# Key-matrix products of an attention and expert kernel in three passes of rounded parts

## Chip, cores and metric

The kernel runs on one core of a Trainium2 chip. The metric is device time in microseconds (us) of one execution; lower is better. A core has five engines that run side by side, each through its own list of instructions in order: TensorE (PE; its weight loads are listed as PEld), VectorE (DVE), ScalarE (ACT), GpSimd (POOL), and SyncE (SP), which here only issues DMAs. They wait for each other through semaphores.

## The reference

Four batches of 1024 tokens of width 256 attend to 77 context rows each with 16 heads of 64; then a mixture of 9 experts (the best two per token) follows. Cut to what matters for this change:

```python
xn = layernorm(x, ln1_w, ln1_b)            # x: the context rows, 4 x 77 x 256
ln = layernorm(latents, ln2_w, ln2_b)      # latents: the normed tokens, 4 x 1024 x 256
q = ln @ Wq
k, v = jnp.split(xn @ Wkv, 2, axis=-1)
q = q * (1.0 + scale) + shift              # one scale and one shift for each batch and head
attn = softmax(einsum('bihd,bjhd->bhij', q, k) * 64 ** -0.5)
x = x + einsum('bhij,bjhd->bihd', attn, v) @ Wout
x = x + experts(layernorm(x))              # top 2 of 9, gate, up and down products
```

## The kernel before

All data are float32. Where products run on parts, a matrix is held as a rounded high part (type F32R) and the rest, its low part (also F32R), and `product` (L338 to L342) sums high x high, high x low and low x high, three matmuls.

The token side of the scores never forms q. Since q is linear in the normed token, Wq and the keys are multiplied beforehand into a key matrix `keymat` of 256 rows for each batch, head and context row, and the scores of a token tile are one product with it. In the same way v and Wout are multiplied into value matrices, which go through DRAM (`valmat_dram`) because they are needed in another layout. This preparation fills the first 75 us or so; then come 32 token tiles (`step(s, s)`, L1429), then the experts. The order of each engine's work is written out by hand.

The preparation in order, by what PE does:

- Context rows are normed and turned. For each of 8 head pairs c PE makes keys into banks 4 to 7 and values into banks 0 to 3 (L1237 to L1243). ACT copies each value block out (L975, L976; increments `prep_moved`). DVE makes `k_head` from the keys, four operations of 64x308 for each c (L1580, `keys_moved`): for each head, its own 64 rows times the scale, the other 64 rows times the shift. Ahead of pair 4 DVE also makes the matrix `mix` (L1564, L1567).
- PE turns Wout in four groups (L1250), which ACT empties (`empty`, L953). Every block of the phase goes through the banks 0 to 3 in turn, and `fill(n)` waits until ACT has emptied block n-4. The blocks are numbered: values 0 to 7, Wout 8 to 11, query weights 12 to 19.
- PE multiplies Wq by `mix` for each pair (L1259), with small side products (L1264, L1266). ACT moves the result into `wq_head` (L985), each head's own 64 rows; the other 64 rows hold 1/256 from a GpSimd memset (L793). It ends each pair with L988.
- The value and key stage. For m = 0 to 31 PE makes one key matrix block (L1310: one float32 matmul of `wq_head`, 128x128, with `k_head`, 128x308); the first 16 of them each follow a value block `val(m)` (L1283, float32, 64 rows). ACT rounds each key block to `keymat` high (L1022) and DVE subtracts for the low part (L1591); four banks are in turn. ACT and DVE move the value blocks in turn (L1001, L1610) into four staging buffers `val_st`, and SP stores each filled buffer to `valmat_dram` with two or three DMAs (L596). Eight stores are made in this stage. After them SP waits until all are written (L602), issues `load_valmat(0)` (L612, L614), and goes on.
- Eight more value blocks of 52 rows are staged in `late_f` and `valmat_f` (`late_vals`), four in the steps 0 and 1 each; DVE waits for all eight stores to be written before it moves the first (L1607).

Of the kernel before, what the change touches and what calls it, by code (L numbers as in the profile page):

```python
# [28 lines left out]
P = 128  # L29
# [14 lines left out]
BM = B * M  # L44
# [9 lines left out]
STATS_DONE = 4  # L54
VALS_FROM = 4
STORE_HEADS = 4
STORE_BUFFERS = 4
# [60 lines left out]
def program(nc, x, ctx_rows, fside, ln1_w, ln1_b, ln2_w, ln2_b, wq, wkv, wout, wr, wg, wu, wd, out):  # L118
# [3 lines left out]
    with ExitStack() as ctx:  # L122
# [3 lines left out]
        def sb(name, shape, dt=F32, on=ctx):  # L126
            return on.enter_context(nc.sbuf_tensor(name, shape, dt))
# [45 lines left out]
        most = sb("most", [P, E])  # L173

        xn = [sb(f"xn{i}", [P, 2, ROW]) for i in range(4)]
        gap = [sb(f"gap{i}", [P, 1]) for i in range(2)]
# [52 lines left out]

        wq_head = sb("wq_head", [P, PAIRS, 2, D], F32, prep)  # L230
        k_head = sb("k_head", [P, PAIRS, 2, BM], F32, prep)
        early = ExitStack()
        wkv_sb = sb("wkv_sb", [P, KT, 2 * INNER], F32, early)
# [4 lines left out]
        side_row = sb("side_row", [1, B * H], F32, early)  # L238
        c_parts = [sb(f"c_{n}", [P, KT, BM], F32R, early) for n in ("hi", "lo")]
        ln_cols = sb("ln_cols", [P, 4, KT], F32, early)  # L240
# [137 lines left out]
        keys_made = sem("keys_made")  # L378
        keys_moved = sem("keys_moved")
        val_made = sem("val_made")  # L380
        val_moved = [sem(f"val_moved{i}") for i in range(2)]
# [114 lines left out]
        def prep_bank(n):  # L496
            return bank[n % 4]
# [67 lines left out]
        def _(sp):  # L565
# [44 lines left out]
            def load_valmat(b):  # L610
# [3 lines left out]
                sp.dma_start(valmat_f[0:KLAST, b % 2, KC - 1, :], rows[(KC - 1) * P:]).then_inc(valmat_loaded, 16)  # L614

            load_valmat(0)
            for n in range(SOON_STORES, STORES):
# [142 lines left out]
        def _(pool):  # L760
# [31 lines left out]
            pool.wait_ge(wkv_split, len(KV_PIECES))  # L792
            nc.gpsimd.memset(wq_head[:], 1.0 / D).then_inc(halves_filled, 1)  # L793

# [154 lines left out]
        def _(act):  # L949
# [21 lines left out]
            for c in range(PAIRS):  # L971

                act.wait_ge(prep_made, PREP_V + c + 1)
                src = prep_bank(PREP_V + c)
                nc.scalar.activation(v_whole[:, :, c, :], src[:, 0:(CR - 1) * P].rearrange("p (r n) -> p r n", n=P), ACT.Copy)  # L975
                nc.scalar.activation(v_last[:, c, :], src[:, (CR - 1) * P:BM], ACT.Copy).then_inc(prep_moved, 1)  # L976
            for n in range(4):
                half = slice(n % 2 * INNER // 2, (n % 2 + 1) * INNER // 2)
                empty(PREP_OUT + n, wout_t[:, n // 2, half], prep_bank(PREP_OUT + n))
# [229 lines left out]
        def _(pe):  # L1209
# [46 lines left out]
            for c in range(PAIRS):  # L1256
                to = fill(PREP_WQ + c)
                for k in range(KT):
                    nc.tensor.matmul(to[:, 0:D], wq_sb[:, k, c * P:(c + 1) * P], mix[:, k, :],  # L1259
                                     start=k == 0, stop=k == KT - 1)  # L1260
# [10 lines left out]
            def val(m):  # L1271
# [5 lines left out]
                if not m:  # L1277
                    pe.wait_ge(prep_moved, PREP)
                if m >= 2:
                    pe.wait_ge(val_moved[m % 2], (m - 2) // 2 + 1)  # L1280
# [18 lines left out]
            for m in range(MATS):  # L1299
# [8 lines left out]
                if m >= 4:  # L1308
                    pe.wait_ge(mat_lo, m - 3)
                nc.tensor.matmul(mat_bank(m)[:, 0:BM], wq_head[:, h // 2, h % 2, k * P:(k + 1) * P], k_head[:, h // 2, h % 2, :],  # L1310
                                 start=True, stop=True).then_inc(mat_made, 1)
            def scores(s, c, i):
# [192 lines left out]
        def _(dve):  # L1505
# [65 lines left out]
            for c in range(PAIRS):  # L1571
# [3 lines left out]
                for i in range(2):  # L1575
# [3 lines left out]
                    for rows, by in ((own, side_scale), (other, side_shift)):  # L1579
                        ins = nc.vector.tensor_tensor(k_head[rows, c, i, :].rearrange("p (b k) -> p b k", b=B), keys,  # L1580
                                                      by[own, :, 2 * c + i].unsqueeze(2).to_broadcast([DH, B, M]), ALU.mult)
                ins.then_inc(keys_moved, 1)

            def mat_rest(m):
# [483 lines left out]
```

## Time and profile before

| what | us |
|---|---|
| median of 3 timed runs | 855.67 (854.84 to 857.24) |
| the profiled execution, its own time | 854.76 |
| its span, first to last instruction | 853.1 |
| mean granted TensorE clock in it | 0.982 of full speed |

| engine | busy us (share of the span) |
|---|---|
| PE | 805.5 (94%) |
| DVE | 669.4 (78%) |
| ACT | 620.8 (73%) |
| POOL | 368.2 (43%) |

The profile is one execution. Its page gives the busy share of each engine, the clock that the throttle granted to TensorE (1.00 is full speed), the chain of work that ended last, and the costliest groups of instructions. The trace behind it can be asked for one stretch: instructions in order of time, the chain, groups by line and shape, and busy time by window. "Idle before it, releaser" says how long the engine had waited and which instruction's semaphore ended that. A float32 matmul shows as two records; one of an F32R operand as one. A busy share over the whole span is a mean over stages, and the preparation is a small one: what is read for this change is the first 92 us.

### The profile page before, as it was taken

What the parts mean: (1) busy time and instruction counts of PE and PEld (TensorE: products, weight loads), DVE (VectorE), ACT (ScalarE), POOL (GpSimd) and SP (SyncE); (2) the same over time, 40 slices, a digit from 0 to 9 for tenths busy, and PEclk for the clock granted to TensorE, in tenths of its full rate; (3) what the DMA queues carried; (4) which work ended last, traced back from release to release, by engine and by line L of the source; (5) the groups of instructions that cost most, each with busy time, mean ns of one, the idle gap of its engine ahead of it and who ended that gap; (6) DMA issues with size and microseconds to landing.
All of it is one profiled execution on the core that took longest, in us unless ns stands there. A gap on an engine that the chain in (4) does not pass through costs nothing.

```text
span 853.1 us, 19506 instructions
## 1 busy us (share of the span) xinstructions
PE 805.5 (94%) x6007; PEld 761.1 (89%) x6007; DVE 669.4 (78%) x1624; ACT 620.8 (73%) x1959; POOL 368.2 (43%) x534
## 2 busy tenths in 40 slices
PE   5999999999999999789699999999999999999993
PEld 4846899999999999789699999999999999999993
DVE  6667888889888887878578778888787888888771
ACT  4557989899889888535477777778777777777771
POOL 3020268677778766652133334233333222523232
PEclk9999999999999999879899999999999999999998
DMA  8044720310320020647547247246745565555212
GB/s 290 10 120 147 227 82 32 121 56 32 104 72 33 33 82 33 199 125 180 143 100 192 45 103 188 39 106 187 186 112 148 140 155 148 143 143 154 46 25 26
DMA packets 77675, 96.14 MB, mean 113 GB/s; under 512 B 10311, under 2 KB 64771, under 8 KB 77571
## 3 DMA queue, kind: packets, MB, share of 16 engines
q1 hardware_dynamic: 63811, 75.93, 29.4%
q0 software_dynamic: 13760, 18.96, 11.7%
q8 instruction: 48, 0.79, 0.4%
q14 instruction: 56, 0.46, 0.2%
HBM read 108.14 MB, written 31.29 MB: 163 GB/s over the span
## 4 chain that ended last, share of the span: by engine, by line
PE 84%; DMA 5%; SPq 3%; issue 2%; DVE 2%; ACT 1%; POOL 1%; DVEq 0%; POOLq 0%; ACTq 0%
PE banks L340 24%; PE banks L342 24%; PE banks L341 24%; PE banks L1327 4%; DMA valmat_dram<-val_st 2%; PE banks L1478 2%; PE banks L1341 2%; DMA expert_in<-blank 1%; SPq L596 1%; PE banks L1259 1%; PE banks L1283 1%; DMA tok<-expert_in 1%; PE banks L1295 1%; PE banks L1310 1%; DMA wkv_sb<-in_L_xattn_Wkv 0%
## 5 line engine op out<-in xcount | busy, mean ns | idle before, releaser
L340 PE MATMUL banks<-tok_t_hi,wgt_hi 128*128 128x256 f32 x704 | 202.2, 287 | 2.9 <-DVE hid_f L1947 2.5
L342 PE MATMUL banks<-tok_t_hi,wgt_lo 128*128 128x256 f32 x704 | 200.6, 285 | 0.0
L341 PE MATMUL banks<-tok_t_lo,wgt_hi 128*128 128x256 f32 x704 | 200.2, 284 | 0.0
L932 POOL DMA_INDIRECT result<-res,tok_id x72 | 117.6, 1634 | 184.5 <-ACT res L1162 154.0
L1032 ACT ACTIVATE prob<-banks,row_min 128x77 f32<-128x77 f32 x512 | 161.7, 374 | 5.7 <-DVE row_min L1674 5.7
L1939 DVE TENSOR_TENSOR wgt_lo<-wgt,wgt_hi 128x704 fp32r<-128x704 f32 x174 | 150.3, 904 | 14.7 <-ACT wgt_hi L1105 14.7
L340 PEld LDWEIGHTS banks<-tok_t_hi,wgt_hi 128*128 128x128 f32 x704 | 135.6, 193 | 5.3 <-issue 3.9
L341 PEld LDWEIGHTS banks<-tok_t_lo,wgt_hi 128*128 128x128 f32 x704 | 135.7, 193 | 0.0
L342 PEld LDWEIGHTS banks<-tok_t_hi,wgt_lo 128*128 128x128 f32 x704 | 135.6, 193 | 0.0
L1105 ACT ACTIVATE wgt_hi<-wgt 128x704 fp32r (+1 forms) x174 | 130.5, 800 | 0.5
L1032 ACT ACTIVATION_READ_ACCUMULATOR prob<-banks,row_min 128x1 f32 x512 | 130.7, 257 | 0.0
L340 PE MATMUL banks<-wgt_hi,hid_hi 128*128 128x256 f32 x360 | 105.0, 292 | 7.4 <-issue 6.1
L342 PE MATMUL banks<-wgt_hi,hid_lo 128*128 128x256 f32 x360 | 102.0, 283 | 0.0
L341 PE MATMUL banks<-wgt_lo,hid_hi 128*128 128x256 f32 x360 | 101.5, 282 | 0.0
L882 POOL TENSOR_TENSOR prob<-prob,row_inv 128x1232 f32<-128x1232 f32 x32 | 72.1, 2253 | 56.5 <-DVE row_inv L1688 56.4
L340 PE MATMUL banks<-valmat_hi,prob_t_hi 128*128 128x266 f32 x320 | 95.1, 297 | 0.7 <-DVE logits L1696 0.7
L341 PE MATMUL banks<-valmat_lo,prob_t_hi 128*128 128x266 f32 x320 | 92.3, 289 | 0.0
L342 PE MATMUL banks<-valmat_hi,prob_t_lo 128*128 128x266 f32 x320 | 92.2, 288 | 0.0
L869 POOL DMA_INDIRECT expert_in<-xn,top_slot x64 | 67.7, 1057 | 39.0 <-POOL xn L859 24.9
L340 PEld LDWEIGHTS banks<-wgt_hi,hid_hi 128*128 128x128 f32 x360 | 68.9, 191 | 9.6 <-DVE wgt_lo L1939 5.3
L921 POOL COPY tok_gate<-tok 128x2 f32<-128x2 f32 (+1 forms) x40 | 17.8, 446 | 131.0 <-DMA result<-res,tok_id 131.0
L340 PE MATMUL banks<-keymat_hi,zn_t_hi 128*128 128x462 f32 (+1 forms) x192 | 73.2, 381 | 0.0
(269 smaller groups left out, 2101.3 us busy)
## 6 DMA issues: line engine op xcount, KB each, us to landing
wgt<-in_L_ffn_Wg SPq DMA_DIRECT2D x29, 704.0 KB
wgt<-in_L_ffn_Wu SPq DMA_DIRECT2D x29, 640.0 KB
wgt<-in_L_ffn_Wd SPq DMA_DIRECT2D x29, 640.0 KB
tok<-expert_in SPq DMA_DIRECT2D x32, 258.0 KB, 2.9
spare_wgt<-in_L_ffn_Wg SPq DMA_DIRECT2D x9, 704.0 KB, 4.4
spare_wgt<-in_L_ffn_Wu SPq DMA_DIRECT2D x9, 640.0 KB, 6.6
spare_wgt<-in_L_ffn_Wd SPq DMA_DIRECT2D x9, 640.0 KB, 6.8
valmat_f<-valmat_dram SPq DMA_DIRECT2D x4, 1197.0 KB, 6.3
```

The source lines that it names most:

```text
L340: nc.tensor.matmul(to, a[0], b[0], start=first, stop=False)
L341: nc.tensor.matmul(to, a[0], b[1], start=False, stop=False)
L342: return nc.tensor.matmul(to, a[1], b[0], start=False, stop=last)
L869: nc.gpsimd.indirect_dma_start(expert_in, bass.IndirectOffsetOnAxis(ap=top_slot[c % 4][:, k:k + 1], axis=0), xn[c % 4][:, k, :], None).the ...
L882: nc.gpsimd.tensor_tensor(p, p, row_inv[i][:].unsqueeze(2).to_broadcast([P, H, M]), ALU.mult).then_inc(prob_ready, 1)
L921: nc.gpsimd.tensor_copy(tok_gate[i][:, 0:blocks], tok[i][:, 0:blocks, GATE])
L932: nc.gpsimd.indirect_dma_start(out, bass.IndirectOffsetOnAxis(ap=tok_id[i][:, a:a + 1], axis=0), res[i][:, a, :], None, compute_op=ALU.add ...
L1032: ins = nc.scalar.activation(prob[c % 2][:, h * M:(h + 1) * M], bank[i][:, (h - h0) * M:(h - h0 + 1) * M], ACT.Exp, bias=row_min[c % 2][:, ...
L1105: nc.scalar.activation(wgt_hi[half_of(t)][:, p0:p1], src[:, p0:p1], ACT.Copy).then_inc(weights_hi, 1)
L1327: mm = nc.tensor.transpose(bank[3 + (c * NG + g) % 2][0:n, (m - c0) * P:(m - c0 + 1) * P], prob[c % 2][:, m * P:m * P + n], ident[:])
L1341: mm = nc.tensor.transpose(turned_tokens(t)[:, k, a * P:(a + 1) * P], tok[i][:, a, k * P:(k + 1) * P], ident[:])
L1939: nc.vector.tensor_tensor(wgt_lo[i][0:rows, p0:p1], src[0:rows, p0:p1], wgt_hi[i][0:rows, p0:p1].bitcast(F32), ALU.subtract).then_inc(weig ...
```

## The change

The key matrix product of L1310 becomes three matmuls on parts.

- ACT rounds each pair's `k_head` into `k_hi` (128x616) right behind its copies of value block c, in the same loop, after a wait for `keys_moved`.
- GpSimd subtracts for `k_lo`, which lies over `k_head` (the subtraction is in place).
- ACT writes `wq_head` rounded, and DVE subtracts for `wq_lo` out of the bank, each head's own 64 rows only (1/256 has no rest). PE waits for it before it refills such a bank, and before the first value block.
- The memset of `wq_head` fills the same value as an integer pattern.
- `k_hi` takes new space, so that the load of the first value matrix would come down on it; SP waits for all 32 key products before `load_valmat(0)`.
- `c_hi`, `c_lo` and `wq_lo` lie where `xn` lies later.

```diff
+        wq_lo = sb("wq_lo", [P, PAIRS, D], F32R, lows)
-        wq_head = sb("wq_head", [P, PAIRS, 2, D], F32, prep)
+        wq_head = sb("wq_head", [P, PAIRS, 2, D], F32R, prep)
+        shared = ExitStack()
+        k_lo = sb("k_lo", [P, PAIRS, 2, BM], F32R, shared)
+        shared.close()
         k_head = sb("k_head", [P, PAIRS, 2, BM], F32, prep)
+        k_hi = sb("k_hi", [P, PAIRS, 2, BM], F32R, prep)
...
+            sp.wait_ge(mat_made, MATS)
             load_valmat(0)
...
-            nc.gpsimd.memset(wq_head[:], 1.0 / D).then_inc(halves_filled, 1)
+            nc.gpsimd.memset(wq_head[:].bitcast(U32), ONE_OVER_D).then_inc(halves_filled, 1)
+            for c in range(PAIRS):
+                pool.wait_ge(keys_hi, c + 1)
+                nc.gpsimd.tensor_tensor(k_lo[:, c], k_head[:, c], k_hi[:, c].bitcast(F32), ALU.subtract).then_inc(keys_split, 1)
...
                 nc.scalar.activation(v_last[:, c, :], src[:, (CR - 1) * P:BM], ACT.Copy).then_inc(prep_moved, 1)
+                act.wait_ge(keys_moved, c + 1)
+                nc.scalar.activation(k_hi[:, c], k_head[:, c], ACT.Copy).then_inc(keys_hi, 1)
...
                 to = fill(PREP_WQ + c)
+                if c >= 4:
+                    pe.wait_ge(wq_split, c - 3)
...
                     pe.wait_ge(prep_moved, PREP)
+                    pe.wait_ge(wq_split, PAIRS)
...
-                nc.tensor.matmul(mat_bank(m)[:, 0:BM], wq_head[:, h // 2, h % 2, k * P:(k + 1) * P], k_head[:, h // 2, h % 2, :],
-                                 start=True, stop=True).then_inc(mat_made, 1)
+                c, i = h // 2, h % 2
+                own = slice(i * DH, (i + 1) * DH)
+                d = slice(k * P, (k + 1) * P)
+                to = mat_bank(m)[:, 0:BM]
+                pe.wait_ge(keys_split, c + 1)
+                nc.tensor.matmul(to, wq_head[:, c, i, d], k_hi[:, c, i, :], start=True, stop=False)
+                nc.tensor.matmul(to, wq_head[:, c, i, d], k_lo[:, c, i, :], start=False, stop=False)
+                nc.tensor.matmul(to, wq_lo[own, c, d], k_hi[own, c, i, :], start=False, stop=True).then_inc(mat_made, 1)
...
+            for c in range(PAIRS):
+                dve.wait_ge(prep_moved, PREP_WQ + c + 1)
+                for i in range(2):
+                    own = slice(i * DH, (i + 1) * DH)
+                    ins = nc.vector.tensor_tensor(wq_lo[own, c, :], prep_bank(PREP_WQ + c)[own, 0:D], wq_head[own, c, i, :].bitcast(F32),
+                                                  ALU.subtract)
+                ins.then_inc(wq_split, 1)
```

## Rows read from the trace of the kernel before

**Rows 1.** The page: the chain that ended last, its shares by engine.

```profile
PE 84%; DMA 5%; SPq 3%; issue 2%; DVE 2%; ACT 1%; POOL 1%; DVEq 0%; POOLq 0%; ACTq 0%
```

**Rows 2.** The chain, 43 to 92 us: start us, length us, what.

```profile
43.19 0.72 PE banks L1283 x4
43.91 0.72 PE banks L1310 x2
44.62 0.65 PE banks L1283 x4
...
54.48 0.48 SPq L596
...
56.45 7.87 DMA valmat_dram<-val_st
...
71.16 8.63 DMA valmat_dram<-val_st
...
79.91 0.71 DVE late_f L1610
```

**Rows 3.** Instructions of SP in order of time, 40 to 90 us.

```profile
46.31 25.84 SPq L596 DMA_DIRECT2D valmat_dram<-val_st  x20
79.87 0.38 SPq L612 DMA_DIRECT2D valmat_f<-valmat_dram  x1
```

**Rows 4.** PE in order of time: key blocks alone; then their line (min/median/max ns).

```profile
64.35 1.56 PE L1310 MATMUL banks<-k_head,wq_head 128*128 128x308 f32 x5
...
L1310 PE MATMUL banks<-k_head,wq_head x64: 422/423/527, 43.8 to 73.7; 128*128 128x308 f32 x64
```

**Rows 5.** PE in order of time: products on rounded parts of the same width.

```profile
18.09 0.30 PE L340 MATMUL banks<-c_hi,wkv_hi 128*128 128x308 f32 x1
18.23 0.30 PE L341 MATMUL banks<-c_lo,wkv_hi 128*128 128x308 f32 x1
```

**Rows 6.** DVE and ACT in order of time: keys, last value copy, turned Wout.

```profile
20.73 0.48 DVE L1580 TENSOR_TENSOR k_head<-banks,side_shift 64x308 f32<-64x308 f32 x1
29.27 0.39 ACT L975 ACTIVATE xs<-banks 128x256 f32<-128x256 f32 x1 [1.49 <-PE banks L342]
29.70 2.06 ACT L953 ACTIVATE wout_t<-banks 128x512 f32<-128x512 f32 x4
...
35.89 0.48 DVE L1580 TENSOR_TENSOR k_head<-banks,side_shift 64x308 f32<-64x308 f32 x1
```

**Rows 7.** PE and ACT in order of time: the query weights, first and last pair.

```profile
31.82 0.61 PE L1264 MATMUL banks<-wr_sb,ones 128*128 128x10 f32 x4
...
42.87 0.18 ACT L988 ACTIVATE xs<-banks 128x10 f32<-128x10 f32 x1
```

**Rows 8.** Groups of ACT by shape, whole span: roundings from SBUF (busy us, mean ns).

```profile
L1140 ACT ACTIVATE hid_hi<-hid_f 128x512 fp32r<-128x512 f32 x64 | 40.3, 630 | 28.3 <-DVE hid_f L1947 28.3
...
L1105 ACT ACTIVATE wgt_hi<-spare_wgt 128x704 fp32r<-128x704 f32 x32 | 23.4, 780 | 0.0
```

**Rows 9.** GpSimd and DVE in order of time; then a group by shape, 100 to 800 us.

```profile
15.32 3.57 POOL L793 MEMSET wq_head<- 128x4096 f32 x1 [8.71 <-DVE wkv_lo L1537]
15.35 3.59 DVE L1556 TENSOR_SCALAR side_shift<-side 128x64 f32<-128x64 f32 x1
...
27.86 0.60 DVE L1567 TENSOR_SCALAR mix<-ident,ln_cols,q_mix 128x128 f32<-128x128 f32 x2
...
L882 POOL TENSOR_TENSOR prob<-prob,row_inv 128x1232 f32<-128x1232 f32 x30 | 67.6, 2253 | 23.7 <-DVE row_inv L1688 23.6
```

**Rows 10.** Busy time by window, 79 to 85 us; the last three: clock, DMA share, GB/s.

```profile
79.00:80.00 1.00, 0.00 (x0) 0.00 (x0) 0.09 (x1) 1.00 (x8) 0.00 (x0) 1.00 0.01 4
...
81.00:82.00 1.00, 1.00 (x8) 0.24 (x4) 0.86 (x2) 0.91 (x5) 0.00 (x0) 0.67 0.77 133
84.00:85.00 1.00, 1.00 (x4) 0.85 (x3) 0.01 (x1) 0.00 (x0) 1.00 (x1) 0.63 1.06 319
```

**Rows 11.** DVE in order of time: low parts of the last key blocks.

```profile
69.51 3.85 DVE L1591 TENSOR_TENSOR keymat_lo<-banks,keymat_hi 128x308 fp32r<-128x308 f32 x8 [0.24 <-ACT keymat_hi L1022]
```

More of the change, by code:

```diff
@@ L55 @@
 VALS_FROM = 4
+ONE_OVER_D = 0x3B800000
 STORE_HEADS = 4
@@ L173, in program @@
         most = sb("most", [P, E])
+        lows = ExitStack()
+        wq_lo = sb("wq_lo", [P, PAIRS, D], F32R, lows)
+        lows.close()
+        lows = ExitStack()
+        c_parts = [sb(f"c_{n}", [P, KT, BM], F32R, lows) for n in ("hi", "lo")]
+        lows.close()
         xn = [sb(f"xn{i}", [P, 2, ROW]) for i in range(4)]
@@ L238, in program @@
         side_row = sb("side_row", [1, B * H], F32, early)
-        c_parts = [sb(f"c_{n}", [P, KT, BM], F32R, early) for n in ("hi", "lo")]
         ln_cols = sb("ln_cols", [P, 4, KT], F32, early)
@@ L379, in program @@
         keys_moved = sem("keys_moved")
+        keys_hi = sem("keys_hi")
+        keys_split = sem("keys_split")
+        wq_split = sem("wq_split")
         val_made = sem("val_made")
```

## The prediction

> **What bounds the kernel now.** I began with the page's chain of work. PE holds 84% of it [rows 1]: from about 91 us on PE is the bound nearly without a gap, and nothing there is touched. What is left for this change is the preparation, so I asked for the chain from 43 to 92 us [rows 2]. The reader is to see that it changes hands. It runs through PE from the first value block at 43.19, one value block and one key block in turn (0.65 and 0.72 us, 1.37 together), leaves PE at the fourth store (54.48), and from there is made of store DMAs: one issued at 56.45 that lands 7.87 later and frees a staging buffer, the last one issued at 71.16 that lands at 79.79, and the first late value block, which DVE may move only then (79.91). SP's own list says the same: 20 store DMAs from 46.31 to 72.15, then a wait, and the load of the first value matrix at 79.87 [rows 3]. So the key blocks are on the path only in the stretch to 54.48. What sets the path is when the first value block starts; the stores follow from that by their own pace.
>
> **The change part by part.**
>
> *The key products (PE).* A float32 key block with no value block beside it: five records take 1.56 us; less the last one's own 0.42 that is 1.14 for four spacings, 0.285 each, and two records are a block, 0.57 us [rows 4]. Beside a value block it is 0.72 [rows 2], so 0.15 goes into each change between a 128-row and a 64-row matmul. Three matmuls on parts are 0.14 each (18.09 to 18.23) [rows 5], so 0.42. The nominal gain is 0.72 - 0.42 = 0.30 for a block, 9.6 us for 32. Little of it is on the path. Up to the fourth store eight value blocks and seven key blocks pass; the third product has 64 rows, so the 0.15 of a change stays, and the gain is 7 x 0.15 = 1.05 at most if only the bare products count. SP's issues, which are busy for part of that time, take some of it. I take -0.4 for this term; its ends are -1.6 and +0.3. Past the fourth store, DVE already makes one low part each 0.48 us at the end (3.85 for 8) [rows 11], so faster products gain nothing there.
>
> *The rounding of the keys (ACT).* This is the large term. The new wait stands in ACT's loop over the value blocks, so behind it on ACT are queued the copy of the next value block, then the four Wout blocks, then the query weights; and PE waits for ACT's copies in order to refill banks 0 to 3. DVE finishes the keys of pair 0 at 21.21 and those of pair 7 at 36.37, about 2 us a pair [rows 6]. ACT was done with the last value copy long before, near 29.8, and with the four Wout blocks at 31.76 [rows 6]. Now it may round pair 7 only from 36.4. A 128x616 rounding is an estimate between 128x512 (0.63) and 128x704 (0.78) [rows 8]: 0.70. That ends at 37.1; the copy of value block 7 stands ahead of it, behind pair 6, and is on time. The four Wout blocks follow, 2.06, and end at 39.2 instead of 31.76: +7.4. PE can't run ahead: block 12 (the first query weights) needs block 8 emptied, at 37.8, and its side product L1264 needs all four, as it does now at 31.82 [rows 7]. From L1264 to the last L988 the work is the same, 31.82 to 43.05. So +7.4 for the first value block.
>
> *The clock.* PE now has almost nothing to do from about 30 to 37.8 (its Wout groups, freed one by one). In this trace PE stood still in the whole window 79 to 80; behind that the granted clock fell, 0.67 in the mean of 81 to 82, and was on its way back in 84 to 85 at 0.63 [rows 10], so some 3 us lay at half. A gap several times as long should drop it too, from 2.4 to 1.2 GHz. If the same stretch lies on the query weights, PE loses half of about 4 us since its return, less what the wait for the fourth Wout block covers (0.4 of it): +1.6. Ends: 0 (no drop) and +2.5.
>
> *The low query weights (DVE).* For pairs 0 to 6 two subtractions lie beside the 1.4 us that a pair takes (31.82 to 43.05 for 8) [rows 7]. For pair 7 they stand between L988 and the first value block. The nearest rows are the 64x308 operations at 0.48 [rows 6]; for 256 columns 0.42, two of them and a hop: +0.9, between 0.8 and 1.0. The cover for the others is gone only if DVE is late, and DVE is idle from 36.4 on.
>
> *The low keys (GpSimd).* 616 columns are half of 1232 at 2.25 us [rows 9]: 1.15 each, one for each 2 us of keys, the last done by 38.4, well ahead of the first product. But GpSimd and DVE can hold each other up: DVE's L1556, a 128x64 operation, took 3.59 us beside the 3.57 us memset, and ended with it [rows 9]. The low keys of pair 3 would start near 27.9, right into DVE's L1567 at 27.86 [rows 9], which stands ahead of the keys of pairs 4 to 7. Cost 0 if DVE comes first, 1.2 if not, and then all of it goes into the large term. I take 0. The Trainium skill, SBUF — State Buffer, section "Who interferes with whom", calls this an exclusive lock and says that only one pair of ports is contended; by it the other DVE operations here, which read a bank, are safe, and the sum is the same save for this 1.2.
>
> *The later load (SP).* The wait for all key products stands where SP waits for the stores anyway, until 79.8; the products end near 73 now [rows 11]. It costs nothing while products end ahead of stores. Queued behind it are late stores and the token loads; all move with the stores. The memset is the same 3.6 us, and the moved tiles cost nothing.
>
> **Sum.** +7.4 + 1.6 + 0.9 - 0.4 = +9.5 at the first store's pace. Behind it the stores, the late value blocks and step 1 hang on each other, and from 91 us PE runs without a gap, so nothing gives it back. Against the profiled execution's own 854.76 that makes 864.3; against the median, 0.9 above it, 865.2.
>
> **Rivals.**
>
> *Faster: the key products were the path.* If the chain's PE part held up to the last key block (73.4) [rows 11] and ACT's new wait were covered, 9.6 us less 0.9 would be won: 847. For it speaks that DVE's low parts follow PE's blocks closely up to there. Against it, the stores' last landing at 79.79 and that ACT empties the banks PE needs. It decides only if PE could do the query weights ahead of ACT's empties, which `fill` forbids. Chance 0.05.
>
> *No change: the shift is real but absorbed.* It would need the stores to run 8 us faster, since the landing of 7.9 to 8.6 us is queueing [rows 2] that shorter production turns around. Nothing shows a gap that large in SP's 25.84 us of issues [rows 3]. 855 to 858, chance 0.05.
>
> *Same cause, no clock loss.* The clock stays full or its low stretch falls into the wait: 863.6 and with the -1.6 end 862. Chance 0.25.
>
> *Slower still: PE becomes the last.* Each later key block then has two changes of row count, 0.42 + 0.30 = 0.72 instead of 0.57, over 16 blocks +2.4, and they would end within reach of the stores. PE stands for about 1 us ahead of DVE's release at 79.91 [rows 2, 10], which covers part of it, so at most +1.5; with the 1.2 of the lock and another clock drop, 868 or so. Chance 0.15. The Trainium skill, TensorEngine Tiling (Array Packing), section "Key Properties", says that changing the tiling mode drains TensorE, and it bears on this one; by it the third product costs more than its 0.14. The trace's 0.15 agrees.
>
> The forecast case, 863.6 to 867 with the clock drop, has the remaining 0.50.
>
> **How the numbers follow.** Likeliest 865.2. The range takes in the ends of the unknown costs: low 860.5 (+7.4 + 0.8 + 0 - 1.6, less 1.8 if the clock drop at 81 us does not come this time), high 869 (+7.4 + 2.5 + 1.0 + 1.2, with some of PE's +1.5). The cases outside are the first two rivals and a tail on either side, 2 in 10. A measurement of this kernel can tell about 0.3% (2.6 us) from no change: faster 0.06, same 0.05, slower 0.89.
>
> **What would show it.** Right: ACT's L953 group ends near 39 us, with idle time in ACT released by DVE's k_head; PE idle between 29 and 38; half clock behind it; the first value block near 53; the last early store landing near 89; the window from 92 us on unchanged but shifted. Key products at 0.14 spacing. Wrong: the first value block near 45, which would mean that the keys come earlier than I think, or a store train much shorter than 33 us.

## The result and the profile after

| what | before | after |
|---|---|---|
| median, us | 855.25 (853.00 to 857.24) | 883.87 (883.42 to 895.47) |
| ratio to before | | 1.0373, 95% interval 1.0313 to 1.0432 |
| the profiled execution, its own time | 854.76 | 883.95 |
| its span | 853.1 | 882.3 |
| mean granted TensorE clock in it | 0.982 | 0.959 |

The kernel is slower by 28.6 us; the forecast was +9.5. The quotient of the two medians is 1.0335, within the interval of the ratio. Three of the four times of after lie between 883.4 and 884.0 with a mean clock of 0.959 to 0.961, the fourth is 895.5 with 0.943: clock and time go together.

The page of the kernel after, its first lines and the shares of its chain; they answer to [rows 1].

```profile
PE 826.0 (94%) x6039; PEld 775.3 (88%) x6039; DVE 678.9 (77%) x1640; ACT 625.5 (71%) x1967; POOL 385.6 (44%) x542
...
PE 82%; DVE 5%; DMA 4%; issue 3%; SPq 2%; POOL 2%; ACT 1%; DVEq 0%; POOLq 0%; ACTq 0%
```

PE is busy for 20.5 us more with only 32 records more (three for a key block instead of two). Even at 0.4 us each they would be 13 us: a part of its work must have run at the other clock level.

The chain of the kernel after, 37 to 57 us (start us, length us, what); it answers to [rows 2] and [rows 7].

```profile
37.17 0.49 DVE k_head L1609
37.68 0.72 ACT k_hi L996
38.40 0.49 ACT wout_t L971
39.03 2.04 PE banks L1281 x4
...
42.59 1.90 PE banks L1281 x4
...
47.70 1.59 PE banks L1281 x4
...
49.65 0.96 PE banks L1281 x4
...
55.91 0.42 DVE wq_lo L1617
...
56.91 0.72 PE banks L1306 x4
```

The handover is the predicted one: the last keys, ACT's rounding, Wout, then the query weights. The same line L1281 takes 1.90 us for a pair at 42.59 and 0.96 from 49.65 on: the first half of the query weights ran at half clock. The first value block is at 56.91 instead of 43.19, +13.7.

PE of the kernel after in order of time, 73 to 80 us.

```profile
73.99 0.41 PE L1338 MATMUL banks<-k_hi,wq_head 128*128 128x308 f32 x1
74.24 0.30 PE L1339 MATMUL banks<-k_lo,wq_head 128*128 128x308 f32 x1
74.47 0.41 PE L1340 MATMUL banks<-k_hi,wq_lo 64*128 64x308 f32 x1
76.24 1.26 PE L1306 MATMUL banks<-xs 64*128 64x266 f32 x4 [1.36 <-ACT val_st L1021]
77.42 0.63 PE L1338 MATMUL banks<-k_hi,wq_head 128*128 128x308 f32 x1
77.85 0.46 PE L1339 MATMUL banks<-k_lo,wq_head 128*128 128x308 f32 x1
```

PE stops for 1.36 us, because a staging buffer is not free yet, and behind the stop the same instructions take 0.63 and 0.46 us instead of 0.41 and 0.30. Busy time by stretch shows for how long (PEclk, the third number from the end, is the granted clock):

```profile
core 0: us, PE busy (x) PEld busy (x) DVE busy (x) ACT busy (x) POOL busy (x), PEclk, DMA share, GB/s
70.00:75.00 5.00, 4.88 (x27) 2.69 (x24) 3.33 (x9) 1.65 (x4) 3.56 (x10) 1.00 0.57 155
75.00:80.00 5.00, 3.76 (x12) 2.09 (x13) 2.77 (x7) 2.19 (x5) 0.00 (x0) 0.62 0.55 159
80.00:85.00 5.00, 5.00 (x12) 2.82 (x11) 1.93 (x4) 1.29 (x3) 0.00 (x0) 0.50 0.40 119
...
105.00:110.00 5.00, 4.76 (x25) 3.58 (x23) 2.72 (x6) 3.19 (x20) 0.00 (x0) 0.81 0.74 248
```

From 80 to 105 us PE is busy in every microsecond, and the clock stays at 0.50 (1.2 GHz of 2.4). It returns only within the score products, near 107. The key blocks end at 103.17, where before they ended at 73.77, and SP shows that they are the last now; this answers to [rows 3]:

```profile
60.13 26.01 SPq L610 DMA_DIRECT2D valmat_dram<-val_st  x20
103.34 0.38 SPq L626 DMA_DIRECT2D valmat_f<-valmat_dram  x1
```

The issues of the stores take 26 us as before (25.84). Before, their last landing came 33.5 us behind the first issue; at that pace the load would have been due near 93.7. It starts at 103.34, right behind the last key product, 9.6 us later, by the wait that was to cost nothing.

So the 29.2 us of the two spans lie as follows. Up to the first value block: +13.7. From there to the first score product: 46.3 us (56.91 to 103.17) instead of 30.6 (43.19 to 73.77), +15.7. From there to step 2 (L1327 at 91.14 before, L1356 at 119.18 after) -1.4, and +1.2 over all the rest.

### The profile page after: what moved, and what is told of

Same layout as the page of the kernel before. It is cut to its first block, busy times and chain, and to the rows that moved or that the text cites. A ratio compares the mean times of both kernels' runs of the same rounds, so it can differ in the third digit from the quotient of the medians.

```text
span 882.3 us, 19634 instructions
## 1 busy us (share of the span) xinstructions
PE 826.0 (94%) x6039; PEld 775.3 (88%) x6039; DVE 678.9 (77%) x1640; ACT 625.5 (71%) x1967; POOL 385.6 (44%) x542
## 3 DMA queue, kind: packets, MB, share of 16 engines
q1 hardware_dynamic: 63811, 75.93, 28.6%
## 4 chain that ended last, share of the span: by engine, by line
PE 82%; DVE 5%; DMA 4%; issue 3%; SPq 2%; POOL 2%; ACT 1%; DVEq 0%; POOLq 0%; ACTq 0%
PE banks L351 23%; PE banks L353 22%; PE banks L352 22%; PE banks L1356 4%; PE banks L1507 2%; DVE k_head L1609 2%; PE banks L1370 2%; PE banks L1340 1%; PE banks L1338 1%; PE banks L1281 1%; DMA expert_in<-blank 1%; DMA valmat_dram<-val_st 1%; PE banks L1306 1%; PE banks L1318 1%; DMA tok<-expert_in 1%
## 5 line engine op out<-in xcount | busy, mean ns | idle before, releaser
L939 POOL COPY tok_gate<-tok 128x2 f32<-128x2 f32 (+1 forms) x40 | 23.7, 591 | 131.5 <-DMA result<-res,tok_id 131.5
```

The costliest lines, as they stand in the source:

```text
L939: nc.gpsimd.tensor_copy(tok_gate[i][:, 0:blocks], tok[i][:, 0:blocks, GATE])
```

## The experiments

Where these kernels have the three products, their lines are shifted by a few numbers against the kernel after. One table first, read from PE's and SP's lists of each profiled run; "stage" is the time from the first value block to the first score product, "load" the start of the load of the first value matrix. Each kernel was timed beside runs of before of its own, whose medians were 854.78 (e1, e2, e3, e5), 854.01 (e9, e4, e6, e7) and 853.31 (e10, e12); the ratio is against those.

| kernel | first value block | stage | load | median, us | ratio (interval) |
|---|---|---|---|---|---|
| before | 43.19 | 30.6 | 79.87 | 855.25 | 1 |
| after | 56.91 | 46.3 | 103.34 | 883.87 | 1.0373 (1.0313 to 1.0432) |
| e9_act_wait_alone | 56.13 | 30.8 | 93.06 | 867.32 | 1.0135 (1.0102 to 1.0169) |
| e1_f32_product | 58.47 | 33.2 | 96.50 | 866.73 | 1.0147 (1.0126 to 1.0169) |
| e2_roundings_moved | 49.94 | 58.4 | 108.54 | 887.86 | 1.0385 (1.0365 to 1.0406) |
| e3_third_128_rows | 55.58 | about 44 | 99.93 | 878.31 | 1.0276 (1.0261 to 1.0290) |
| e4_mix_first | 58.27 | 57.3 | 115.73 | 893.72 | 1.0442 (1.0406 to 1.0479) |
| e5_filler | 59.96 | 50.9 | 111.05 | 888.0 | 1.0383 (1.0360 to 1.0405) |
| e10_two_more | 59.53 | 45.7 | 105.41 | 881.01 | 1.0308 (1.0281 to 1.0335) |
| e6_paired | 43.59 | 37.2 | 80.68 | 857.39 | 1.0040 (1.0011 to 1.0070) |
| e7_paired_spread | 43.71 | 28.3 | 79.58 | 855.71 | 1.0013 (0.9995 to 1.0031) |
| e12_stores_on_two | 43.64 | 36.5 | 82.02 | 860.20 | 1.0084 (1.0068 to 1.0100) |

Each stage is read from one execution, and where the clock falls and returns differs from one execution to the next. In after, e1, e3, e5 and e10 the query weights are the same instructions of PE and begin between 38.9 and 39.5, at half clock in all five. Full clock was back at 48.9 in after, 52.0 in e1, 46.2 in e3, 54.7 in e5 and 54.1 in e10, so that their first value blocks lie between 55.58 and 59.96, nearly all of it by this. Differences of a few us between two of these kernels are not to be explained by their edits. What does hold in every execution is the mean clock of the whole: 0.937 to 0.961 in all 20 runs of after, e2, e3, e4 and e5, and 0.970 to 0.978 in all 12 of e1, e9 and e10.

**ACT's wait alone.** The kernel before with nothing of the change that costs time but the rounding on ACT, its wait, and SP's wait (the places in memory and the integer memset are those of after); the key products stay float32.

```diff
                 nc.scalar.activation(v_last[:, c, :], src[:, (CR - 1) * P:BM], ACT.Copy).then_inc(prep_moved, 1)
+                act.wait_ge(keys_moved, c + 1)
+                nc.scalar.activation(k_hi[:, c], k_head[:, c], ACT.Copy).then_inc(keys_hi, 1)
```

> The kernel before with one thing of the change: ScalarE rounds each pair's keys in its loop over the value blocks, behind the wait for VectorE's keys (the rounded keys are not used). No low parts, float32 key blocks. By the sum of the prediction, with the clock as seen since: the four turned Wout blocks end near 39 instead of 31.8, the query weights run at half clock for some 8 us, and the first value block starts near 53 to 54 instead of 43.2, so the time is 854.8 + 10 = 865, within 862 to 867. Against the kernel that keeps all but the three-pass product (866.7) this leaves 2 us for GpSimd's hold on VectorE and the low query weights. Rival (the low parts and GpSimd's lock make the late start, not the wait): the time is within 3 us of 855.

The copies of Wout on its ACT, then its PE, in order of time:

```profile
36.89 2.04 ACT L968 ACTIVATE wout_t<-banks 128x512 f32<-128x512 f32 x4
...
37.61 2.04 PE L1276 MATMUL banks<-mix,wq_sb 128*128 128x256 f32 x4 [1.06 <-ACT wout_t L968]
...
56.13 0.72 PE L1300 MATMUL banks<-xs 64*128 64x266 f32 x4 [1.14 <-ACT xs L1005]
```

The copies of Wout end at 38.93 instead of 31.76: +7.2, the +7.4 of the forecast. The first value block is 12.9 us late; the other 5.8 are the clock, which is at half here from 33.5 to 50.6. One wait costs +13.3 against the runs of before beside it, with its clock loss. The stage behind it is unchanged (30.8). The value block is 2 to 3 us behind the expected 53 to 54, by the clock, and the time just above the expected range.

**All of the change but the product.** One float32 matmul for a key block; all roundings of the keys, subtractions and waits stay (`wq_head` stays float32, and GpSimd writes over `k_hi`, so that `k_head` is left for the product).

```diff
-                nc.tensor.matmul(to, wq_head[:, c, i, d], k_hi[:, c, i, :], start=True, stop=False)
-                nc.tensor.matmul(to, wq_head[:, c, i, d], k_lo[:, c, i, :], start=False, stop=False)
-                nc.tensor.matmul(to, wq_lo[own, c, d], k_hi[own, c, i, :], start=False, stop=True).then_inc(mat_made, 1)
+                nc.tensor.matmul(to, wq_head[:, c, i, d], k_head[:, c, i, :], start=True, stop=True).then_inc(mat_made, 1)
```

> Everything of the change is kept (roundings on ScalarE with their wait, GpSimd's and VectorE's low parts, the wait on SP), but the key block is again one float32 matmul, so the parts are computed and not used. Theory 1 (two separate costs: the late start by ScalarE's wait, and a key stage at half clock that the three-pass product brings): the first value block still starts near 57, the stage from it to the scores takes 31 to 32 us at full clock instead of 46, and the time is 855.3 + 13.7 = 869, within 867 to 871. Rival (the half clock is an after-effect of PE's long gap near 30 to 38, whatever product is used): the stage stays at half clock for long stretches and the time stays above 878.

Its granted clock by stretch, in the columns of the view of after:

```profile
60.00:65.00 5.00, 5.00 (x13) 2.01 (x12) 2.33 (x5) 1.44 (x4) 0.00 (x0) 0.50 0.20 59
65.00:70.00 5.00, 5.00 (x22) 2.01 (x22) 3.15 (x7) 2.10 (x6) 0.00 (x0) 0.93 0.39 112
```

The clock fell here as well, early in the stage, but it was back after 6.8 us of float32 blocks (58.8 to 65.7), and the stage takes 33.2 us. The time is 0.3 us below the range of theory 1, and the rival is out. With the same delay ahead of it, the product on parts is worth about +17 us (866.73 to 883.87). Most of that lies in half clock, and what the three products do to the clock is what has to be found.

**The roundings moved.** ACT rounds pairs 0 to 3 four pairs later in its loop, and pairs 4 to 7 in the key stage, between its copies, so that its wait no longer stands ahead of the query weights.

```diff
-                act.wait_ge(keys_moved, c + 1)
-                nc.scalar.activation(k_hi[:, c], k_head[:, c], ACT.Copy).then_inc(keys_hi, 1)
+                if c >= 4:
+                    round_keys(c - 4)
...
+                if m < 8 and m % 2:
+                    round_keys(4 + m // 2)
```

> The changed kernel with ScalarE's eight roundings taken out of the way: those of pairs 0 to 3 stand four pairs later in its loop over the value blocks, where their keys are ready, and those of pairs 4 to 7 in the key stage behind the first key blocks. Theory 1: the first value block starts at 44 to 45 (the low query weights' 0.9 us stay), 12 to 13 us earlier than in the changed kernel; the key stage still loses its clock and takes about 46, so the time is 870 to 872. Rival (the gap near 30 to 38 is what upsets the clock later): with the gap gone the key stage runs at full clock, 30 us or less, and the time is 854 to 857.

PE of this kernel in order of time:

```profile
39.19 2.04 PE L1288 MATMUL banks<-mix,wq_sb 128*128 128x256 f32 x4 [1.90 <-DVE wq_lo L1624]
...
49.94 1.26 PE L1313 MATMUL banks<-xs 64*128 64x266 f32 x4 [2.03 <-DVE wq_lo L1624]
```

The path moved to DVE: `wq_lo` of pair 0 stood behind all of `k_head` (to 38.18), and PE waited 1.90 us for it. The clock fell, the value block came at 49.94, 7 us earlier than in after, and yet the kernel is slower: it lay at 0.50 from 49.4 to 110.9, and the stage took 58.4 us. The expected time was missed by 16 us. This was a strong sign that the three-product stage itself keeps the clock down; a start 7 us earlier is worth less than the state in which it begins.

**The third product with 128 rows.** Its weights are 128 rows of zeros instead of the 64 of `wq_lo`, so that this part is left out of the result.

```diff
-                nc.tensor.matmul(to, wq_lo[own, c, d], k_hi[own, c, i, :], start=False, stop=True).then_inc(mat_made, 1)
+                nc.tensor.matmul(to, zeros[:], k_hi[:, c, i, :], start=False, stop=True).then_inc(mat_made, 1)
```

> The changed kernel, but the third matmul of a key block has a 128x128 block of zeros as weights and all 128 rows of the rounded keys, so the low query weights' part is left out of the result; it takes the place of the 64-row one in form only. It tells whether the change of row count inside each block is what keeps the clock at half. Theory 1a (the changes of row count are it): key blocks beyond the 16th run 0.42 to 0.5 us apart, the clock comes back within some 4 us after PE's stop near 75, the stage takes about 30 us instead of 46, and the time is 866 to 870. Theory 1b (any series of short rounded products does it): the clock stays at half to the scores, blocks are 0.8 us apart, and the time is 876 or more.

PE in order of time, about the end of the value blocks:

```profile
88.67 1.26 PE L1308 MATMUL banks<-xs 64*128 64x266 f32 x4
89.85 0.62 PE L1340 MATMUL banks<-k_hi,wq_head 128*128 128x308 f32 x1
90.27 0.46 PE L1341 MATMUL banks<-k_lo,wq_head 128*128 128x308 f32 x1
90.53 0.46 PE L1342 MATMUL banks<-k_hi,zeros 128*128 128x308 f32 x1
...
93.87 0.37 PE L1340 MATMUL banks<-k_hi,wq_head 128*128 128x308 f32 x1
94.08 0.30 PE L1341 MATMUL banks<-k_lo,wq_head 128*128 128x308 f32 x1
```

While a value block of 64 rows stood between, the clock was 0.50, for 33 us (from 56.5). The value blocks end at 90; from there on only 128-row products follow each other, 0.26 us apart, and 4.1 us later the clock is back, and they are 0.14 apart. In the kernel after, where each key block holds a 64-row product, it did not come back in the same place (80 to 103). Neither theory came out whole: the blocks alone behaved as 1a says, but the stage took 44 us and the time is in the range of 1b. The value blocks kept the changes of row count, and the stream of products around them thin, so this run does not tell one from the other.

**A dense filler.** 14 further 128-row products into the bank of key block 14, which the block then overwrites.

```diff
+                if m == 14:
+                    pe.wait_ge(mat_lo, m - 3)
+                    for _ in range(14):
+                        nc.tensor.matmul(mat_bank(m)[:, 0:BM], wq_head[:, 6 // 2 + 0, 0, 0:P], k_hi[:, 3, 0, :], start=True, stop=True)
```

> The changed kernel with 14 more matmuls (128 rows, 0.14 us each, overwritten by the block that follows) ahead of the 15th value block, where PE stopped for 1.4 us near 75 waiting for a staging buffer. Theory 2 (that stop is what makes the clock fall, and the sparse product then doesn't bring it back): the clock stays at 2.4 GHz through the key stage, blocks without a value block are 0.6 to 0.75 us apart, and the time is 870 to 873. Rival (the 64-row change alone lets the clock fall, stop or no stop): the clock falls a few us later anyway and the time stays within 3 us of 884.

```profile
90.53 3.96 PE L1332 MATMUL banks<-k_hi,wq_head 128*128 128x308 f32 x14
94.42 1.26 PE L1306 MATMUL banks<-xs 64*128 64x266 f32 x4
95.61 0.41 PE L1342 MATMUL banks<-k_hi,wq_head 128*128 128x308 f32 x1
...
97.70 0.41 PE L1342 MATMUL banks<-k_hi,wq_head 128*128 128x308 f32 x1
...
98.52 0.41 PE L1342 MATMUL banks<-k_hi,wq_head 128*128 128x308 f32 x1
```

The clock had fallen at 61.5, 29 us ahead of the filler, so neither the expected time nor its rival was tested (888 against 870 to 873, or within 3 us of 884). The rows do tell something: 29 us at half ahead of the filler; the 14 products 0.28 us apart, still at half; the value block behind them at half too (1.26 us); and full clock from 95.6 on, 5.1 us behind the filler's start and 1.1 behind its end. It stays full for the 15 us to the end, although the blocks are again those of the kernel after, 0.81 us apart. Those blocks, then, can hold the clock, and did not regain it in 29 us.

**Two more products in each key block.** The kernel after, with more work in every block.

```diff
+                for _ in range(2):
+                    nc.tensor.matmul(to, wq_head[:, c, i, d], k_hi[:, c, i, :], start=True, stop=True)
                 nc.tensor.matmul(to, wq_head[:, c, i, d], k_hi[:, c, i, :], start=True, stop=False)
```

> The changed kernel with more work in it: ahead of the three products of each key block, two further 128-row products of the same operands go to the same bank, and the block's first product overwrites them. PE does five matmuls in a key block instead of three, nothing else differs. Theory 1 (the clock stays at 1.2 GHz because the stream of blocks around it is too thin for it to come back; float32 blocks and long runs of 128-row products did bring it back): the clock returns within some 5 us behind each fall, a key block beside a value block takes about 1.5 to 1.6 us at full clock instead of the 2.2 to 2.3 that it takes at half, the way from the first value block to the scores is 33 to 37 us instead of 46, and the time is 868 to 876, less than the 884 of the changed kernel though it does more. Theory 2 (the clock stays low for a reason that more work does not touch, the time of the stops in it or their number): each block grows by about 0.5 us at half clock, 32 blocks by up to 16, and the time is 890 to 900.

PE in order of time: the fall, the return, and blocks alone near the end. Then the clock by stretch.

```profile
60.95 1.50 PE L1306 MATMUL banks<-xs 64*128 64x266 f32 x4
62.38 0.88 PE L1339 MATMUL banks<-k_hi,wq_head 128*128 128x308 f32 x2
...
69.41 0.55 PE L1339 MATMUL banks<-k_hi,wq_head 128*128 128x308 f32 x2
...
103.06 0.55 PE L1339 MATMUL banks<-k_hi,wq_head 128*128 128x308 f32 x2
103.45 0.30 PE L1340 MATMUL banks<-k_hi,wq_head 128*128 128x308 f32 x1
103.59 0.30 PE L1341 MATMUL banks<-k_lo,wq_head 128*128 128x308 f32 x1
103.82 0.40 PE L1342 MATMUL banks<-k_hi,wq_lo 64*128 64x308 f32 x1
104.15 0.55 PE L1339 MATMUL banks<-k_hi,wq_head 128*128 128x308 f32 x2
```

```profile
65.00:70.00 5.00, 5.00 (x23) 3.37 (x22) 2.53 (x6) 1.95 (x4) 0.00 (x0) 0.72 0.30 91
70.00:75.00 5.00, 5.00 (x31) 3.23 (x31) 2.96 (x8) 2.04 (x5) 0.00 (x0) 1.00 0.56 159
```

The clock fell near 61 and was back at 67.8, 6.8 us later, and stayed at 1.00 to the end of the stage. With 64 products more than the kernel after the stage took 45.7 us instead of 46.3. Theory 2 is out, and the rows are those of theory 1; but the two added products make the stream denser and also put more 128-row products between two changes of row count, and no run separates these. Its figures for stage and time were wrong through my own arithmetic: 16 blocks at 1.55 (with their value block) and 16 at 1.10 are 42.4 at full clock, not 33 to 37. What the blocks grew by was paid for by the clock: the kernel does more and is no slower than after (1.0308 against 1.0373, with intervals that overlap), although its first value block came 2.6 us later (the query weights lay at half clock until 54 instead of 49).

The rows at 103 also price a block by its parts at full clock: a 128-row product behind another 0.14 (103.45 to 103.59), the 64-row product 0.23 behind its predecessor, the next block 0.33 behind that, and the second product of a block 0.25 behind the first (0.39 for two spacings, less 0.14). A block of three is 0.25 + 0.23 + 0.33 = 0.81, which is what e5 shows (97.70 to 98.52).

**`mix` ahead of the low keys.** GpSimd waits for `mix` before it makes the low keys of pair 3, so that the two no longer meet.

```diff
+                if c == 3:
+                    pool.wait_ge(mix_made, 1)
```

> The changed kernel, but GpSimd holds back the low keys of pair 3 until VectorE has made mix, the operation that took 1.8 us instead of 0.6 with GpSimd beside it. Theory (GpSimd's operation holds VectorE up): VectorE's two mix operations of L1596 take 0.6 us again, the keys of pairs 4 to 7 are 1.2 to 1.3 us earlier, and the first value block starts 1 to 1.3 us earlier, near 55.7. The whole time is no clean witness, since where the clock falls later moves it by more: 870 to 890. Rival (the operation is slow for another reason): it stays at 1.8 us and the first value block at 56.9.

GpSimd (its `k_lo` of pair 3) and DVE of the kernel after, in order of time:

```profile
27.90 1.50 POOL L811 TENSOR_TENSOR k_lo<-k_head,k_hi 128x616 fp32r<-128x616 f32 x1 [0.47 <-ACT k_hi L996]
```

```profile
27.92 1.82 DVE L1596 TENSOR_SCALAR mix<-ident,ln_cols,q_mix 128x128 f32<-128x128 f32 x2
```

DVE of this kernel:

```profile
28.02 0.60 DVE L1598 TENSOR_SCALAR mix<-ident,ln_cols,q_mix 128x128 f32<-128x128 f32 x2
```

GpSimd starts 0.02 us ahead of DVE, and two operations that take 0.60 us elsewhere [rows 9] take 1.82: +1.2. With the meeting gone they take 0.60 again. The cause is settled. The query weights begin 1.1 us earlier for it (37.91 instead of 39.03), but the first value block is not at the expected 55.7: it came at 58.27, since the clock lay at half in the query weights until 52.8. It fell again at 59.6 and stayed at half to 121.1, past the end of the stage, and the time of 893.7 is above the expected 870 to 890.

**Key blocks in pairs.** Both heads of a pair together: four 128-row products in a row, then the two of 64 rows in the two halves of the rows; with it the moved roundings and `wq_lo` of pair 0 ahead of the last keys on DVE. The second version also spreads the value blocks, the last 8 of them one for each pair of key blocks instead of two.

```diff
+                for i in range(2):
+                    nc.tensor.matmul(to, wq_head[:, c, i, d], k_hi[:, c, i, :], start=True, stop=False)
+                    nc.tensor.matmul(to, wq_head[:, c, i, d], k_lo[:, c, i, :], start=False, stop=False)
+                for i in range(2):
+                    nc.tensor.matmul(mat_bank(m + i)[:, 0:BM], wq_lo[own, c, d], k_hi[own, c, i, :], start=False, stop=True).then_inc(mat_made, 1)
```

> A three-pass version with the waits taken out of the way: ScalarE's roundings moved as before (none waits), GpSimd's low keys behind mix, the low query weights' first pair ahead of the last keys on VectorE, and key blocks made two at a time: the two 64-row products of a pair of heads, on rows 0 to 63 and 64 to 127, come last and run side by side, so that a pair of blocks has one change of row count each way instead of two. Theory (changes of row count and stops are what costs the clock): the first value block starts near 44, two key blocks without value blocks take 1.0 to 1.1 us at full clock (1.62 in the changed kernel, 1.14 in float32), and the time is 853 to 858 if the clock holds. Rival (three-pass products leave the clock at half once it has fallen, and PE still stops for a staging buffer near 62): the stage from the first value block to the scores takes 38 us or more and the time is above 862.

> The version in pairs, with value blocks 8 to 15 spread out, one for each two key blocks instead of one for each, so that PE has key blocks to make while the stores free the staging buffers. Theory (a stop of PE is what makes the clock fall, and the sparse stage doesn't bring it back): no stop of over 1 us between the first value block and the scores, full clock through the stage, 28 to 31 us for it, and a time of 851 to 856, at or below the kernel before. Rival (the stores set the path, PE's order doesn't): the time is that of the version in pairs without the spread, within 2 us.

PE of the second version, in order of time; then its SP.

```profile
80.31 2.02 PE L1320 MATMUL banks<-xs 64*52 64x266 f32 x8 [3.38 <-DVE late_f L1668]
```

```profile
46.12 25.93 SPq L612 DMA_DIRECT2D valmat_dram<-val_st  x20
79.58 0.38 SPq L628 DMA_DIRECT2D valmat_f<-valmat_dram  x1
```

The first value block is at 43.7, as before, and two key blocks take 1.10 us, less than the 1.14 of two float32 ones. The clock fell at 45.5, in the first microseconds of the stage, and was back by 49. The stage is 2.3 us shorter than before, and the time is the same: PE then stands 3.38 us where it stood 1.84 (78.83 to 80.67), the clock behind that stop lies at half for 6.8 us (79.6 to 86.4) instead of 3.4 (81.3 to 84.7), and the load starts at 79.58 where it started at 79.87. With the delay gone, the train of stores is the path and faster key products gain nothing.

In the first version PE stopped 2.9 us for a staging buffer in mid-stage and paid 16.7 us at half clock, behind which the products ended with the stores. Its stage of 37.2 us is just short of the rival's 38, and yet the median of 857.4 is in the range of the theory: five of its ten times lie between 852.5 and 855.8 with a mean clock of 0.978 or more, the other five, with the profiled one, between 859.0 and 861.6 with 0.976 or less. Up to the first key blocks both versions have the same instructions, and at 45.5 the clock fell in one and not in the other.

**Every second store from GpSimd**, on top of the second version.

```diff
-            for n in range(SOON_STORES):
+            for n in range(0, SOON_STORES, 2):
                 store_vals(n)
...
+            pool_store(1)
+            pool_store(3)
```

> The version with paired key blocks and spread value blocks (855.7), with every second of the eight stores of this stage issued by GpSimd instead of SyncE, each issuer waiting for its own; the work of PE, ACT and DVE is the same. Theory 1 (the path of the preparation is the train of store DMAs on one queue, 33.5 us from the first issue to the last landing, with PE standing 3.4 us for it): two queues shorten the train to 25 to 29 us, PE goes from the last key block to the scores nearly without a stop, and the time is 850 to 853. Theory 2 (the train is as long as it is because of the DMA engines behind the queues, or because GpSimd takes over 1 us for each issue): the last store lands as late as before or later, and the time is 855 to 862.

GpSimd in order of time:

```profile
55.33 4.36 POOL L824 DMA_DIRECT2D valmat_dram<-val_st  x6
...
76.32 2.00 POOL L824 DMA_DIRECT2D valmat_dram<-val_st  x3 [5.59 <-DVE val_st L1690]
```

Its first store stood behind the last low keys, to 55.33, and the rest moved with it; its last one was issued from 76.32. So PE stood 7.1 us for a staging buffer (59.1 to 66.2), and the clock was at half from 60.9 to 71.1, which is the stage of 36.5 us. The train got 2.4 us longer (load at 82.02) and the kernel 4.5 slower. The time is in the range of theory 2, for a reason that it does not name. Whether two queues are faster than one isn't told by this, since the second one began late.

## Why the prediction was wrong

Direction and first cause were right; the size was not, 883.9 against a range that ended at 869.

- **The rounding on ACT, +7.4:** right. The copies of Wout end at 40.35 instead of 31.76, +8.6: 7.4 for this wait and 1.2 for the next point. In e9, without the latter, it is +7.2. A 128x616 rounding took 0.72 (estimate 0.70).
- **Keys and GpSimd, taken as 0, end 1.2:** wrong value, right end. It was 1.2 (1.82 less 0.60), shown by e4. GpSimd's operation took 1.51 us, not 1.15. The rows had the two starts within 0.1 us of each other; that was a coin toss and not a zero.
- **The clock in the query weights, +1.6, ends 0 and +2.5:** mis-sized. In after it cost the rest of the 13.7: less 8.6 and 0.9 that is +4.2; in e9 it is 5.8. I had taken the 3 us of [rows 10] as the length of any low stretch. It lasted until 48.9, 10 us from the first query weights on; with the same instructions it lasted 7 us in e3 and 15 in e5 and e10. No row gave that length, and a single execution doesn't give it either.
- **The low query weights, +0.9:** right, 0.86 for the pair, and PE waits 2.03 instead of 1.14.
- **The key products, -0.4:** near right beside a value block, where the two take 1.27 us together instead of 1.37 (57.56 to 58.83 in after), a gain of 0.10 where I had 0.15. Wrong for a block alone: it is 0.81 at full clock, more than float32's 0.57. I had let one 0.15 stay beside a value block and priced both changes of a block alone only in a rival, at 0.30 where they cost 0.39. At full clock the stage would be 16 x 1.27 + 16 x 0.81 = 33.3, which is 2.5 more than e9's 30.8 and not less, nearly that rival's +2.4.
- **"It costs nothing while products end ahead of stores":** the step that failed most. The condition was the right one and it broke. 46.3 less 33.3 is 13 us: 1.4 for the stop, the rest for the half clock from 76.2 on. It broke by the clock and not by the price of the products: a stage of 33.3 us would have ended at 90.2, ahead of the stores' 93.7, and the load would not have been the 9.6 us later that it was. The rival in which PE becomes the last had the place right, at a chance of 0.15, but capped it at +1.5, because its clock drop was a short one. It also took PE's wait ahead of DVE's release as about 1 us, where the trace of before has 1.84.
- **Nothing gives it back:** right; the rest of the kernel moved as a block (-1.4 and +1.2).

What I missed was one question: if the clock falls in the new code, what there will bring it back? The rows of before held only stages that recover.

What stays open: why some stops cost the clock and others not. In after 2.03 us at 54.9 did not and 1.36 us at 74.9 did; in e1, e3, e4, e5 and e10 the 2.03 us of the same place were followed by half clock within 2 us of PE's return. And at 45.5 the clock fell in e7 and not in e6, behind the same instructions. That PE had worked too briefly at full clock ahead of the stop is no answer either: in e3 it had since 46 us, in after only since 49. Open too is what in the three-product stage keeps the clock low: that it does is seen in five kernels (after, e2, e3, e4, e5), but whether it is the changes of row count or the thin stream of products no run separates. Nor did a run time the three-product stage at full clock throughout with blocks as in after; its 33.3 is worked out.

## What to carry to other kernels

Price a wait by what is queued behind it on its engine, and then ask of each stop that it makes on PE which work follows, and whether that work has brought the clock back in any trace you have. A stage of short products with changing row counts can be busy in every microsecond and stay at 1.2 GHz; group the products by row count, as e7 does, where two 64-row products also run side by side (0.55 us for a block instead of 0.81). And before making PE faster, look at which transfer ends the stage: here 33.5 us of stores made the best version equal to before. Profile more than one execution where the clock is in play: between runs of the same instructions it returned up to 8 us apart.

## What was not expected of the hardware

- TensorE stayed at 1.2 GHz for 31 us in after (76.2 to 106.9), 61 in e2 and in e4, 37 in e3 and 34 in e5, with hardly any idle time in its records. It came back after 4.1 us of 128-row products in a run (e3), 5.1 us behind the first of 14 of them (e5), 6.8 us when each block had two more (e10), 6.8 us of float32 blocks (e1), and 2.5 to 5.5 us into the score products (e2, after, e4).
- The length of such a stretch is not fixed by the instructions: in the query weights it ended 7 us (e3) to 15 us (e5, e10) behind their start.
- Three products of which one has 64 rows take 0.81 us at full clock; three of 128 rows in a run take 0.42 (0.14 each, in the rows of e3 from 94.08 on, and already in [rows 5]). One odd row count among them costs nearly as much as the three.
- DVE's 128x128 operations took three times as long beside a GpSimd subtraction that had begun 0.02 us earlier (1.82 against 0.60 for two). That agrees with the exclusive lock of the Trainium skill, SBUF — State Buffer, section "Who interferes with whom".
